# Layer 0's attention: the late score products moved directly behind their mask on TensorE

## The reference, cut to what matters

```python
x = L0_attn_h                                   # 16 x 256 x 128
xn = _layernorm(x)
x = x + _L0_attn_ref(xn, Wqvk, Wo) + _L0_ffn_ref(xn, ...)
xn = _layernorm(x)
x = x + _L1_attn_ref(xn, ...) + _L1_ffn_ref(xn, ...)

def _L0_attn_ref(h, Wqvk, Wo):                  # 16 heads of 8
    qvk = (h @ Wqvk).reshape(b, s, 3, H, HD)
    q, v, k = qvk[:, :, 0], qvk[:, :, 1], qvk[:, :, 2]
    scores = einsum('bshi,bthi->bsth', q, k)
    scores = scores + causal_mask               # -inf above the diagonal
    weights = softmax(scores / sqrt(d), axis=2)
    wv = einsum('bsth,bthi->bshi', weights, v).reshape(b, s, d)
    return wv @ Wo
```

## Time and profile before

| | us |
|---|---|
| median of 3 runs (783.6 to 785.65) | 784.93 |
| span of the profiled execution | 765.3 |
| outside the span (the difference of the two) | 19.6 |
| TensorE busy | 703.9 (92%) |
| VectorE busy | 546.6 (71%) |
| ScalarE busy | 419.5 (55%) |
| GpSimd busy | 327.7 (43%) |

### The profile page before, as it was taken

How to read it: one execution, slowest core, us unless ns; L and a number is a source line. 1 busy time by engine, 2 the same in 40 slices (tenths; PEclk the granted TensorE clock), 3 DMA queues, 4 the chain that set the end, 5 groups by cost and what they waited for, 6 DMA issues and landing times.

```text
span 765.3 us, 17690 instructions
## 1 busy us (share of the span) xinstructions
PE 703.9 (92%) x6133; PEld 526.3 (69%) x6133; DVE 546.6 (71%) x1053; ACT 419.5 (55%) x802; POOL 327.7 (43%) x433
## 2 busy tenths in 40 slices
PE   5787788998899978989898999999999999999997
PEld 4643445556755547757666888888888888888885
DVE  6878997885678866779886766666665666666665
ACT  5645665676477678677664444444444444444442
POOL 3765643783758860147694631212122221222222
PEclk9999999999999999999999999999999999999999
DMA  6984655431134420012114611112121212111100
GB/s 188 261 239 137 179 133 201 167 95 49 51 120 129 142 85 1 12 33 61 54 43 117 156 52 56 56 41 69 41 69 41 69 41 59 50 52 58 41 15 14
DMA packets 63795, 66.51 MB, mean 87 GB/s; under 512 B 6512, under 2 KB 41840, under 8 KB 63728
## 3 DMA queue, kind: packets, MB, share of 16 engines
q1 hardware_dynamic: 62128, 63.23, 27.7%
q0 software_dynamic: 1024, 2.12, 1.0%
q10 hardware_dynamic: 576, 0.27, 0.1%
HBM read 47.46 MB, written 17.99 MB: 86 GB/s over the span
## 4 chain that ended last, share of the span: by engine, by line
PE 75%; DVE 9%; issue 5%; ACT 4%; DMA 3%; POOL 2%; SPq 1%; ACTq 0%; POOLq 0%; DVEq 0%
PE ps L1763 25%; PE ps L1992 22%; PE ps L1876 3%; DVE m L1241 3%; PE ps L1683 3%; PE ps L1587 3%; PE ps L1796 2%; PE ps L1831 2%; PE ps L1593 2%; PE ps L1597 2%; PE ps L1897 1%; DMA qk_parts<-qk_p 1%; PE ps L1601 1%; PE ps L1688 1%; PE ps L1580 1%
## 5 line engine op out<-in xcount | busy, mean ns | idle before, releaser
L963 ACT ACTIVATE f_h<-ps 128x512 fp32r<-128x512 f32 x256 | 153.3, 599 | 197.6 <-PE ps L1763 197.6
L1463 DVE SCALAR_TENSOR_TENSOR f_l<-ps,f_h 128x512 fp32r<-128x512 f32 x256 | 175.9, 691 | 112.5 <-ACT f_h L963 111.3
L1763 PE MATMUL ps<-x_hl,w_h 128*128 (+1 forms) x512 | 200.3, 391 | 0.0
L783 POOL TENSOR_TENSOR acc<-acc,yt 128x512 f32<-128x512 f32 x55 | 70.9, 1289 | 249.8 <-DVE yt L1501 249.8
L877 ACT ACTIVATE probs<-ps 128x1536 f32<-128x1536 f32 x64 | 92.8, 1450 | 34.4 <-PE ps L1606 33.8
L1763 PEld LDWEIGHTS ps<-x_hl,w_h 128*128 128x128 f32 x512 | 96.1, 188 | 19.6
L682 POOL TENSOR_SCALAR_AFFINE_SELECT probs<-probs 128x512 f32<-128x512 f32 x128 | 78.4, 637 | 59.8 <-ACT probs L877 59.5
L1992 PE MATMUL ps<-f_l,w_h 128*128 128x512 f32 x256 | 99.8, 390 | 1.3 <-DVE f_l L1463 1.3
L1992 PE MATMUL ps<-f_h,w_h 128*128 128x512 f32 x256 | 99.7, 390 | 0.0
L1763 PE MATMUL ps<-x_hl,w_l 128*128 (+1 forms) x256 | 99.6, 389 | 0.0
L1992 PE MATMUL ps<-f_h,w_l 128*128 128x512 f32 x256 | 99.6, 389 | 0.0
(11 more groups left out here) (225 smaller groups left out, 1328.2 us busy)
## 6 DMA issues: line engine op xcount, KB each, us to landing
gate_b<-gate_rows SPq DMA_DIRECT2D x64, 256.0 KB, 3.3
qk_parts<-qk_p SPq DMA_DIRECT2D x16, 512.0 KB, 3.8
k_st<-qk_parts SPq DMA_DIRECT2D x64, 96.0 KB
q_st<-qk_parts SPq DMA_DIRECT2D x64, 96.0 KB
y_tok<-zero SPq DMA_DIRECT2D x8, 512.0 KB, 2.9
w_raw<-in_w_e SPq DMA_DIRECT2D x16, 256.0 KB, 2.7
x_rows<-xn_rows SPq DMA_DIRECT2D x8, 260.0 KB, 3.2
w_up<-in_w_up SPq DMA_DIRECT2D x8, 256.0 KB, 2.7
```

What stands on the lines that cost most here:

```text
L783: nc.gpsimd.tensor_tensor(acc[:, :], acc[:, :], yt[:, e % 2, :], ALU.add).then_inc(summed, 1)
L963: nc.scalar.activation(r32(f_h[:, m % 4, :]), ps[:, m % 4, :], ACT.Relu).then_inc(f_hi, 1)
L1463: nc.vector.scalar_tensor_tensor(out=r32(f_l[:, m % 4, :]), in0=ps[:, m % 4, :], scalar=0.0, in1=f_h[:, m % 4, :], op0=ALU.max, op1=ALU.su ...
L1763: last = nc.tensor.matmul(dst, r32(lhs[i]), r32(rhs[j]), start=(k == 0), stop=(k == 2))
```

## The change

The four late products of group n+3 leave `scores` and become a function of their own, `late_scores`, called after `mask_late` and the occasional `attention_out`, `turn_heads` and `find_slots`, and ahead of `turn_out`, `turn_max` and `mask_early`. Their wait for `stack_in` and the increment of `late_done` go with them. No instruction is added or removed, and no other engine's list changes. It applies in slots 0 to 60 (n+3 below 64).

```diff
+            def late_scores(far):
+
+                if at(far, RING) % 2 == 0:
+                    pe.wait_ge(stack_in[at(far, RING) // 2], div(far, RING) * 64 + 64)
+                for n in range(2):
+                    for u in range(2):
+                        last = late(far, u, n)
+                last.then_inc(late_done, 1)
+
             def scores(g):
 
                 far = plus(g, 3)
                 both = within(far, G0)
-                if both:
-                    if at(far, RING) % 2 == 0:
-                        pe.wait_ge(stack_in[at(far, RING) // 2], div(far, RING) * 64 + 64)
-                    for n in range(2):
-                        for u in range(2):
-                            last = late(far, u, n)
-                    last.then_inc(late_done, 1)
                 if past(g, 1):
                     pe.wait_ge(exp_done, num(g))
                 else:
@@ slot
                 if n == FIND:
                     pe.wait_ge(wv_put, FIND - 4)
                     find_slots()
+                if within(plus(g, 3), G0):
+                    late_scores(plus(g, 3))
                 if past(g, 4) and within(plus(g, -4), G0):
                     turn_out(plus(g, -4))
```

## The result

The changed kernel takes 798.65 us (median of 4 runs, 797.18 to 800.9) where the kernel before takes 785.29 us in the runs beside it (783.6 to 787.9). The ratio is 1.0173 with a 95% interval from 1.0144 to 1.0202: **slower by 13.4 us**. Forecast were 801 us and +16.3 us.

What follows compares the result with a forecast made beforehand. VectorE's loop through the output turn and divide bounds many slots, TensorE others; 6.7 + 5.5 + 2.1 + 0.4 + 1.7 + 0.3 - 0.4 = +16.3 us, from 784.9 to 801 us. Range 788 to 807, eight times in ten.

Steps and rivals of the forecast that it cites:

- The delay of 0.42 us: Output turn starts later in each slot: 0.09 us passage, 0.23 us late products, 0.10 us passage back.
- Slots bound by VectorE: Slots 6 to 19, 21 and 22: the divide and next mask move by the full 0.42 us, 16 slots, +6.7 us.
- the rest of VectorE's work follows it: VectorE's work behind the divide L1326 shifts with it, so L1241 and the next mask move by the full 0.42 us.
- Statistics and attention sum: Slots 47 to 51, 53 to 60: +5.5 us; slots 26, 30, 34, 42, 46: +2.1 us; 0.42 us each.
- Slots bound by TensorE: Thirteen head-turn or pre-expert slots plus slot 52: TensorE loses 0.12 us each, +1.7 us; bare slots lose 0.
- the 19.6 us outside the span: Difference between the 765.3 us span and 784.9 us time, taken as constant and added to the forecast span of 781.6.
- Slot 39's lateness: Directly behind the experts, the turn of the maxima, which an exponential follows, is late by 0.42 us: +0.4 us.
- Slot 50's wait for a DMA: TensorE waits 0.40 us for a DMA there, which takes up that much of the delay: -0.4 us.
- The passages cost nothing: Where the late products now stand, only their 0.23 us of columns delay the output turn: 793 us, chance 0.17.
- The early release wins: L1241's 7.5 us wait for the late products L1597 would be gained and the loop shrink: 777 us, chance 0.08.
- The rival that changes nothing: VectorE's idle time in the following slot makes up the divide's delay: 785 us within 0.3%, chance 0.08.
- Worse: Delayed maxima and exponentials push GpSimd's and DMA queue work, or ScalarE loses 0.1 us a slot: 807 us or more, chance 0.10.

Runs made afterwards that it cites:

- the exchange of one pair of lines: Changed kernel with the output turn put back in front of the late products: 785.55 us, ratio 0.9992 to the kernel before.
- the pure delay: Kernel before with two extra copies of the late mask ahead of the output turn in slots 6 to 22: 789.69 us; with four copies 797.99 us.
- the fresh profile of before: Kernel before, unchanged, profiled again beside the other runs: 784.57 us, ratio 1.0004, span 781.5 us.
- the run in the TensorE-bound slots: Kernel before with the change only in slot 20 and the bare and head-turn slots from 23 on: 787.3 us, ratio 1.0034.
- the two runs that should have cost 2 to 3 us: Changed kernel with output turn before late products, 785.55 us; kernel before with late products between turn of the maxima and early mask, 784.74 us.

## Why the prediction was right, point by point

**The mechanism was right.** VectorE's loop over the output turn sets the pace in the marks' slots, and the change pushes it back. The chain above shows it, the exchange of one pair of lines undoes it, and the pure delay reproduces it. The size was less exact than the 801 us look: +16.3 us were forecast and +13.4 measured, with an interval from 11.3 to 15.9. The terms below say where the 3 us went; errors of both signs lie beneath them.

**The delay of 0.42 us was nearly right.** The start of the output turn moved by 0.42; the divide moved by 0.47 to 0.48, because the pair of turns itself got 0.06 us longer.

**Slots bound by VectorE: 6.7 forecast, 5.6 measured** (4.83 + 0.80). Sixteen times 0.47 would be 7.5. The step that was mis-sized is "the rest of VectorE's work follows it": I took that work as fixed. It is not. L1170 and L1177 together took 4.5 + 7.0 us before and 3.0 + 6.2 after, 2.3 us less, while two instructions of slot 6 took 1.08 us more. Neither was forecast, so that 5.6 came out near 6.7 is in part luck.

**Statistics and attention sum: 7.6 forecast** (5.5 + 2.1), **6.7 measured** (4.74 + 1.99) up to slot 59. Slot by slot it was 0.37 to 0.48 us, where 0.42 was forecast. The stretch from the earlier trace rows shows it best; a statistics slot with a head turn (slot 57) in the fresh profile of before:

```profile
274.98 0.39 PE L1587 MATMUL ps<-mask_qk,ident_h 128*128 128x256 bf16 x2
275.32 0.38 PE L1796 MATMUL ps<-ident,o_ring 128*128 128x128 f32 x2
275.74 0.21 DVE L1326 RECIPROCAL rden<-ps 128x8 f32<-128x8 f32 x1 [0.22 <-PE ps L1796]
276.51 1.21 DVE L1241 TENSOR_REDUCE m<-ps 128x4 f32<-128x1024 f32 x1
277.78 0.39 PE L1587 MATMUL ps<-mask_qk,ident_h 128*128 128x256 bf16 x2
```

The same slot in the changed kernel:

```profile
286.91 0.39 PE L1587 MATMUL ps<-mask_qk,ident_h 128*128 128x256 bf16 x2 [0.26 <-DVE m L1241]
287.67 0.44 PE L1800 MATMUL ps<-ident,o_ring 128*128 128x128 f32 x2
288.14 0.21 DVE L1326 RECIPROCAL rden<-ps 128x8 f32<-128x8 f32 x1 [0.69 <-PE ps L1800]
288.92 1.21 DVE L1241 TENSOR_REDUCE m<-ps 128x4 f32<-128x1024 f32 x1
290.18 0.39 PE L1587 MATMUL ps<-mask_qk,ident_h 128*128 128x256 bf16 x2 [0.26 <-DVE m L1241]
```

Counted from the slot's first mask, the output turn moves from 0.34 to 0.76 us, the divide from 0.76 to 1.23, L1241 from 1.53 to 2.01 and the next mask from 2.80 to 3.27. From L1241 to the next mask it is 1.27 and 1.26 us, and the mask now waits 0.26 us for VectorE, where no wait is shown before: the tie is broken, as forecast. What the sum lost against the forecast is in slot 60, which the table does not reach, and in slot 30, where the stops of no named releaser are (4.58 us before, 4.20 after).

**Slots bound by TensorE: +1.7 forecast, about +1.0 measured, +2.6 when alone.** The length 2.90 us was forecast and 2.95 measured; the difference is the same longer pair of output turns. In the sum a shorter stop in slot 36 (4.33 us before, 3.43 after) hides half. The bare slots lose nothing, as forecast. That the engine drains when the tiling mode changes, as "TensorEngine Tiling (Array Packing)" of the Trainium skill says under Key Properties, agrees with these rows: the same products with two more passages take 2.90 us where they took 2.78. The forecast that slots 23 to 37 would be longer by 0.15 us on average was missed: they are longer by 0.4 us in all, 0.03 each, since the shorter stops in slots 30 and 36 hide the rest.

**What was wrong: the 19.6 us outside the span.** I took the difference of the span and the median as time outside the span and added it back. The real figure is 1.9 to 2.3 us. Of the rest, 16.2 us are span that the first profile did not have, 15.5 of them in the stretches named under the fresh profile; stops and a low clock are seen there, but how much each costs was not separated. The 801 us survived this, since what the 19.6 us hold is in both kernels and was added back whole. The terms that were read from the first profile held where its slots are like those of the fresh one, in 6 to 22 and 42 to 59, and there lie 12.5 of the 13.3 us. Slot 39's lateness (+0.4 forecast, -0.06 measured) and the +0.3 for slots 0 to 5 (-0.35 measured) did not come. Slot 50's wait for a DMA, priced at -0.4, is in neither later profile, and slot 50 lost 0.47 us in full (3.47 to 3.94). Slot 40 has a head turn and was in none of the forecast's groups; it changed by 0.03 us.

**The rivals.** "The passages cost nothing" falls by the run in the TensorE-bound slots, and by rows: in slot 24 the weight loads at both passages start together with their first products (144.93 and 145.25), so none is pulled ahead. The prediction had taken only one of the two conditions that "TensorE: Matmul & The Clock Gate" of the Trainium skill gives under "Step-by-step: what each phase is for"; for this place the rows settle it. "The early release wins" falls: its wait did go (8.2 to 2.3 us against the fresh profile) and bought nothing, since the divide was now last. The rival that changes nothing falls with the 13.4 us. "Worse" by GpSimd's or ScalarE's queues being pushed was not seen; GpSimd did cost VectorE 1.08 us in slot 6, by another way.

## What to carry to other kernels

Before you move work ahead of other work on an in-order engine, list who waits for each piece that is pushed back, and ask whether that waiter is the bound in that stretch; a wait of 8 us that shrinks to 2 can be worth nothing while 0.47 us on the right loop costs the kernel 13 us. The cheap test is to exchange the moved piece with its neighbours one by one, and a plain delay in front of the suspected piece shows the slope. Take the profile of before again beside the others, since two profiles of one kernel differed here by 16.2 us, more than the change is worth. Here the piece wanted early was the output turn, not the late products: putting it ahead of the wait gave 4 us.

## What was not expected of the hardware

**VectorE and GpSimd stop each other.** The mark L1170 takes 0.7 us or 1.5 us, by which of the two starts first. In slot 11 of the fresh profile of before GpSimd is first:

```profile
94.01 1.05 POOL L653 TENSOR_TENSOR of_tile<-in_tile,places 128x512 bf16<-128x512 bf16 x1
94.08 1.52 DVE L1170 TENSOR_TENSOR in_tile<-r_s,places 128x512 bf16<-128x512 f32 x1
```

and in the same slot of the run with the output turn in front of the late products VectorE is:

```profile
92.62 0.71 DVE L1170 TENSOR_TENSOR in_tile<-r_s,places 128x512 bf16<-128x512 f32 x1
92.76 1.48 POOL L653 TENSOR_TENSOR of_tile<-in_tile,places 128x512 bf16<-128x512 bf16 x1
```

Whoever is second is longer by about what is left of the first: GpSimd's 1.05 becomes 1.48, VectorE's 0.71 becomes 1.52. The page "SBUF — State Buffer" of the Trainium skill says under "Who interferes with whom" that a VectorE instruction with two SBUF inputs contends with a GpSimd one that reads SBUF, and that contention for the port pair they share is an exclusive lock. These rows agree with the contention. If the second did nothing until the first had ended, they would give 1.69 us for L1170 and 1.62 us for L653, worked out from the rows; 1.52 and 1.48 were measured, so the lock is complete to within some 0.15 us. For a forecast it means that a shift of 0.4 us can give or take 2 us in this stretch (the marks took 2.3 us less in the changed kernel). It is part of why the two runs that should have cost 2 to 3 us came out even: their marks took 0.7 and 0.9 us less than before. The rest of what they gained was not traced.

**One profile need not be one of the timed runs.** The first profile's span is 16.2 us shorter than that of the fresh one, at the same kernel. Its terms were good, but its absolute time was not; the difference between span and time should be taken from the profiled execution's own time, where it is 2 us. What releases the engines after the stops, and why the first execution had fewer of them, was not tried and stays open.
